# Cross-attention and routed FFN on one core: four PSUM copies of the first two batches moved from ScalarE to VectorE, and one key projection placed behind the transposes

## What is computed

```python
qp = q @ Wq.T                                   # q = layernorm(x)
k, v = jnp.split(latent_kv @ Wkv_expand.T, 2, axis=-1)
scores = jnp.einsum('bhqd,bhkd->bhqk', qh, kh) * inv_sqrt_d
scores = jnp.where(causal, scores, jnp.finfo(scores.dtype).min)
attn = jax.nn.softmax(scores, axis=-1)
out = jnp.einsum('bhqk,bhkd->bhqd', attn, vh)   # heads put together
x = x + out @ Wout.T
x = x + ffn(layernorm(x))                       # top-2 of 8 experts, plus the shared part
```

## Time and profile before

| | us |
|---|---|
| median of 3 runs | 339.84 (339.09 to 340.3) |
| the profiled execution | 340.88 |
| its span, first to last instruction | 339.0 |
| TensorE busy in the span | 323.1 (95%) |
| VectorE busy | 268.6 (79%) |
| ScalarE busy | 232.4 (69%) |
| GpSimd busy | 143.3 (42%) |

### The profile page before, as it was taken

One profiled execution on the slowest core, in us unless ns is written; L12 is line 12 of the kernel. 1 busy time (PEld: TensorE's weight loads), 2 busy tenths in 40 slices (PEclk: granted clock), 3 DMA queues, 4 the chain that ended last, 5 costly groups with the idle time before them and its releaser, 6 DMA issues.

```text
span 339.0 us, 7041 instructions
## 1 busy us (share of the span) xinstructions
PE 323.1 (95%) x2285; PEld 279.3 (82%) x2285; DVE 268.6 (79%) x677; ACT 232.4 (69%) x582; POOL 143.3 (42%) x151
## 2 busy tenths in 40 slices
PE   7999998999999999999999999899999999999990
PEld 7898876777786798889888978789989999999980
DVE  4889779999756176876667998899999999999940
ACT  4666999999844134131225788788899899989830
POOL 3335475888842000352500005557772432432463
PEclk9999999999999999999999999999999999999996
DMA  7999300000005699598699965554455455556243
GB/s 227 380 338 380 139 3 3 3 3 3 0 2 198 248 367 370 237 300 289 224 271 253 251 244 98 102 117 104 90 111 131 90 96 125 114 92 113 50 48 45
DMA packets 32227, 53.03 MB, mean 156 GB/s; under 512 B 7488, under 2 KB 15808, under 8 KB 31168
## 3 DMA queue, kind: packets, MB, share of 16 engines
q1 hardware_dynamic: 24912, 43.31, 39.2%
q0 software_dynamic: 4576, 9.23, 15.9%
q10 hardware_dynamic: 2704, 0.04, 0.5%
HBM read 32.24 MB, written 16.92 MB: 145 GB/s over the span
## 4 chain that ended last, share of the span: by engine, by line
PE 74%; ACT 8%; DVE 5%; DMA 5%; POOL 3%; issue 2%; SPq 1%; POOLq 1%; DVEq 0%; ACTq 0%
PE bank L583 26%; PE bank L913 22%; PE bank L940 5%; ACT prob L1076 4%; PE bank L644 3%; PE bank L944 3%; PE bank L807 2%; PE bank L950 2%; PE bank L954 2%; DMA w_sg<-sguT 2%; DMA act_w<-act_e 2%; DMA w_kv<-wkvT 1%; PE bank L793 1%; PE bank L575 1%; PE bank L655 1%
## 5 line engine op out<-in xcount | busy, mean ns | idle before, releaser
L562 POOL DMA_INDIRECT out<-y_sb,dest x18 | 40.6, 2257 | 91.5 <-ACT y_sb L1256 49.7
L1333 DVE TENSOR_TENSOR gu_parts<-w_gu,gu_parts 128x704 fp32r<-128x704 f32 x84 | 76.0, 939 | 0.4 <-ACT gu_parts L1031 0.2
L1031 ACT ACTIVATE gu_parts<-w_gu 128x704 fp32r x84 | 66.1, 792 | 10.8 <-PE bank L913 9.7
L913 PE MATMUL bank<-gu_parts,xsT_hi 128*128 128x352 f32 x328 | 71.1, 338 | 0.0
L913 PEld LDWEIGHTS bank<-gu_parts,xsT_hi 128*128 128x128 f32 x328 | 54.3, 188 | 5.6 <-issue 4.3
L913 PE MATMUL bank<-gu_parts,xsT_lo 128*128 128x352 f32 x164 | 39.6, 323 | 0.0
L583 PE MATMUL bank<-x2T_hi,w_sg_lo 128*128 128x512 f32 (+1 forms) x88 | 32.6, 371 | 0.1
L583 PE MATMUL bank<-x2T_hi,w_sg_hi 128*128 128x512 f32 (+1 forms) x88 | 31.9, 363 | 0.0
L583 PE MATMUL bank<-x2T_lo,w_sg_hi 128*128 128x512 f32 (+1 forms) x88 | 31.9, 363 | 0.0
L445 POOL TENSOR_TENSOR prob<-prob,rrow 112x448 f32<-112x448 f32 x30 | 27.5, 934 | 9.9 <-DVE rrow L1383 9.8
L523 POOL DMA_INDIRECT xs_dram<-x2n,slot_i x14 | 13.9, 993 | 37.6 <-DVE eid L1631 33.6
(11 more groups left out here) (219 smaller groups left out, 826.3 us busy)
## 6 DMA issues: line engine op xcount, KB each, us to landing
w_gu<-guT SPq DMA_DIRECT2D x8, 1408.0 KB, 9.6
xs_dram<-no_row SPq DMA_DIRECT2D x1, 5460.0 KB, 19.7
xs_in<-xs_dram SPq DMA_DIRECT2D x21, 256.0 KB, 10.1
w_dn<-dnT SPq DMA_DIRECT2D x8, 512.0 KB, 7.9
act_w<-act_e SPq DMA_DIRECT2D x19, 176.0 KB, 2.1
w_sg<-sguT SPq DMA_DIRECT2D x10, 256.0 KB
w_dn<-dnT SPq DMA_DIRECT2D x8, 192.0 KB, 8.5
w_sd<-sdnT SPq DMA_DIRECT2D x5, 256.0 KB, 5.8
```

Source lines behind the costliest of these rows:

```text
L562: pool.indirect_dma_start(out=out[:, :], out_offset=bass.IndirectOffsetOnAxis(ap=dest[:, i, 0:1], axis=0), in_=y_sb[i % 2][:, :], in_offse ...
L913: ins = pe.matmul(dst[:, 0:F], xsT[x_][:, c, :], gu2[w_][:, c, f0:f0 + F], start=c == 0 and n == 0, stop=c == C - 1 and n == 2)
L1031: act.activation(dst, src, ACT.Copy).then_inc(s[sem], 1)
L1333: dve.tensor_tensor(lo_, src, hi_.bitcast(F32), ALU.subtract).then_inc(s[sem], 1)
```

## The change

- wait_probT is written anew: copied_by_vector says which copies VectorE makes, now also (batch 0, row 3), (1, 1) and (1, 3); probT_count works out the count of the copy on its semaphore.
- TensorE: k_proj(1, 2) with its wait for kT(1, 1) goes from ahead of transposed(0, 2) to behind transposed(0, 3).
- ScalarE: loses probT 3 of batch 0, probT 1 and 3 of batch 1, and qT(1, 2).
- VectorE, b = 0: qT(1, 2) ahead of inverse(1, 0); then probT 3 and kT(1, 2), both ahead of masked(1, 3); at the end, between inverse(1, 3) and masked(2, 1), probT 1 of batch 1. b = 1: probT 3 directly behind kT(1, 3).

No instruction is added or left out in sum, and no transfer is touched.

```diff
--- before.py
+++ after.py
@@ -266,6 +266,13 @@
 
         "xin0 xin1 xin2 Tx xs_hi xs_lo gu_hi gu_lo dn_hi dn_lo eg esil eact actw Ta aT_hi aT_lo aT dn_last_hi dn_last edn_split edn ey yst ylo yhi").split()
     s = {n: nc.alloc_semaphore(f"s_{n}") for n in names}
+
+    def copied_by_vector(b, r):
+        return r == 1 if b >= 2 else (b, r) in ((0, 3), (1, 1), (1, 3))
+
+    def probT_count(b, r):
+        by = copied_by_vector(b, r)
+        return sum(copied_by_vector(n // R, n % R) == by for n in range(R * b + r + 1))
 
     token_buffer = lambda i: 2 if i == 2 else 1 if i > 2 and i % 2 == 0 else 0
 
@@ -624,12 +631,7 @@
                 transposes(bank_, x2n[:, n, :]).then_inc(s["T2"], 1)
 
             def wait_probT(b, r):
-                if b < 2:
-                    pe.wait_ge(s["probT"], R * b + r + 1)
-                elif r == 1:
-                    pe.wait_ge(s["probT_v"], b - 1)
-                else:
-                    pe.wait_ge(s["probT"], R * 2 + (R - 1) * (b - 2) + (1 if r == 0 else r))
+                pe.wait_ge(s["probT_v" if copied_by_vector(b, r) else "probT"], probT_count(b, r))
 
             def transposed(b, r):
                 if b == 0 and r < RP:
@@ -753,8 +755,6 @@
                 transposed(b, 1)
                 if b == 0:
                     q_proj(1, 2, D)
-                    pe.wait_ge(s["KT"], C + 2)
-                    k_proj(1, 2, CC)
                 if b == 1:
                     pe.wait_ge(s["QT"], C + 3)
                     q_proj(1, 3, D)
@@ -775,6 +775,9 @@
                 if b >= 3:
                     t2(b - 3, CC)
                 transposed(b, 3)
+                if b == 0:
+                    pe.wait_ge(s["KT"], C + 2)
+                    k_proj(1, 2, CC)
                 if b >= 2:
                     out_proj(b - 2, early, 3 * C)
                 if b + 1 < NB:
@@ -1135,15 +1138,12 @@
                     put_qT(1, 0, D)
             for b in range(NB):
                 put_pT(b, 0)
-                if b < 2:
+                if b == 0:
                     put_pT(b, 1)
                 if b + 1 < NB:
                     exps(b + 1, 0)
-                if b == 0:
-                    put_qT(1, 2, D)
                 if b < 2:
                     put_pT(b, 2)
-                    put_pT(b, 3)
                 if b + 1 < NB:
                     exps(b + 1, 1)
                 if b == NB - 1:
@@ -1478,16 +1478,20 @@
             masked(1, 1)
             masked(1, 2)
             for b in range(NB):
+                if b == 0:
+                    put_qT(2, D)
                 if b == 1:
                     put_kT(3)
+                    put_pT(1, 3)
                 if b + 1 < NB:
                     inverse(b + 1, 0)
+                if b == 0:
+                    put_pT(0, 3)
+                    put_kT(2)
                 if b >= 2:
                     put_pT(b, 1)
                 if b + 1 < NB:
                     masked(b + 1, 3)
-                if b == 0:
-                    put_kT(2)
                 if b == 1:
                     put_qT(3, D)
                 if b + 1 < NB:
@@ -1509,6 +1513,8 @@
                     masked(b + 2, 0)
                 if b + 1 < NB:
                     inverse(b + 1, 3)
+                if b == 0:
+                    put_pT(1, 1)
                 if b + 2 < NB:
                     masked(b + 2, 1)
                     masked(b + 2, 2)
```

## The result

The changed kernel took 337.83 us (median of 4 executions, 337.44 to 338.02) against 339.46 (4 executions): ratio 0.9945, 95% interval 0.9926 to 0.9963. That is 1.63 us less by the medians and 1.9 by the ratio, with 1.3 to 2.5 in the interval. It is faster, and more so than forecast: 338.9 was the forecast, and 337.83 lies 0.07 us under the lower end of the range, 337.9, so the forecast was missed. The profiled execution took 337.44 us, with a span of 335.5.

The account below looks back on a forecast made before the run. ScalarE, full in the first two batches, was taken as the bound through its oT_hi of batch 1. A 1.00 us gain there, cut to 0.90 by waiting for transposes, took 339.84 to 338.9 us; range 337.9 to 340.1.

Parts of the forecast that it names:

- starting value: Median of three runs of the kernel before, 339.84 us, from which the sum subtracted the gain.
- lead: ScalarE's exponentials of batch 2, row 1, start 0.90 us earlier, at 46.24 instead of 47.14; bounds 0.60 to 0.95.
- late part: From the first w_gu load to the end of the span; the 0.90 us shift was to be carried through unchanged.
- Part 1: Batches 0 and 1: the copies taken off ScalarE free about 1.8 us, the upper bound of the gain.
- Part 2: Batch 0: k_proj(1,2) behind the transposes lets them start at 37.36; with the copies moved, ScalarE is 1.00 us ahead.
- Part 3: VectorE's new order ends kT(1,2) at 39.59; batch 0's products start at 39.73, 0.30 us earlier; other delays cost nothing.
- Part 4: Batch 1: ScalarE waits 0.95 us for TensorE's transposes before copying row 2, cutting its 1.00 us to 0.90.
- 0.3 us for runs: Allowance for run-to-run variation, added to the terms' bounds to give 338.6 to 339.5 us.
- (a): GpSimd holds up VectorE's three new probT copies, 0.75 us each: 1.35 us slower, 341.2 us; chance 0.06.
- (b): kT(1,2) comes late, or the gain is lost at the w_sg load near 127.99: 339.3 to 339.8 us; chance 0.20.
- (c): Larger gain: TensorE's 1.5 us act_w wait loosens, 337.4 us, or ScalarE's whole 1.8 us counts, 338.0; chance 0.14.
- (d): Batch 0: ScalarE isn't freed, its copies' time returning as waiting for transposes; no own size, chance counted in (b).

Follow-up runs that it names:

- the repeats: The changed kernel, unchanged, against the kernel before, in three more comparisons of 12 executions each: ratios 0.9970, 0.9964 and 0.9972.

## Why the prediction was right or wrong

The mechanism was right for the first two batches and mis-sized a little; the sum built on it failed, in its starting value, in its lead and in what it allowed for runs. The late part, which it took for unchanged, stays open. Times of after are shifted by 0.27 us, the difference of the first exponentials.

| step | before | forecast | after |
|---|---|---|---|
| products of batch 0 | 40.03 | 39.73 | 39.66 |
| transposes of rows 2, 3, batch 1 | 45.53 | 45.23 | 45.11 |
| copy of row 2, batch 1 | 46.30 | 45.82 | 45.69 |
| exponentials of batch 2, row 1 | 47.14 | 46.24 | 46.13 |
| oT_lo of batch 1 | 50.60 | 49.70 | 49.51 |
| first load of w_gu | 104.67 | 103.77 | 103.62 |

**Part 1, ScalarE: right.** A copy costs 0.43 us of the queue (38.27 to 38.70).

**Part 2, the move: right.** In batch 0 the exponentials after the copy start at 38.43 by before's clock (38.70 - 0.27); 38.42 was forecast. What I didn't say, and the runs showed, is that the move has hardly any value without the copies (0.10 alone, about 0.5 on top).

**Part 3, VectorE: right but for one term.** kT(1,2) ends at 39.60 (39.25 + 0.62 - 0.27; forecast 39.59). The products then start 0.06 us later, not 0.13: that hand-over was taken from a transpose that followed a probT copy and is shorter here. The delays that I costed at nothing cost nothing: batch 1's copy of probT 3 was done before its products, and VectorE gated nothing else.

**Part 4, the wait that takes over: right, 0.15 us too long.** ScalarE waits in batch 1 for the transposes, for 0.80 us (free at 44.83 + 0.33 = 45.16, copy at 45.96), not 0.95, mostly since the transposes are 0.12 earlier. The kernel that moves k_proj(1,3) shows that this was the bound that was left. The step after it, that the shift is carried to the end, held in the timed comparisons within their intervals, and not in the profiled executions, whose late parts differ by 1.5 us in the mean.

**The sum, first term that failed: the lead, 0.90 us, was too small by 0.15 to 0.2.** The stage gave 1.05 in the first pair of traces and 1.1 in the mean of five. 0.12 of the difference is the transposes' earlier start: 0.07 the hand-over, and 0.05 the way from products to transposes, 5.45 instead of 5.50 us (39.93 to 45.38). 0.08 more is a term that the sum put at nothing: ScalarE's oT_hi of batch 1 took 0.55 instead of 0.62 us, and VectorE waits for its end.

**Second and third: the starting value and the 0.3 us for runs.** The sum began at 339.84, a median of three. The same kernel was at 339.46 in the comparison with the result, 0.38 lower, and at 339.3 to 340.0 in the larger ones; the changed one was there at 338.25 to 338.5. So a median of three or four can be off by more than the 0.3 us that the range allowed. The forecast is 0.4 to 0.65 above the larger medians of after, and 1.07 above the first measurement. Of these 1.07, 0.38 is the starting value and 0.2 the lead. The remaining 0.5 is what the first comparison gave beyond the stage (1.63 us, where 36 executions gave 1.05); the repeats point to chance, and a small late gain isn't excluded. The range itself would have held every larger median. The first measurement fell on the faster side, to which I gave 0.36, against 0.58 for no change; an effect of 1.05 us lies just at the 0.3% that I took as the border.

**The rivals.** (a), VectorE's copies held up by GpSimd: no. The copy at 46.43 took 0.61 us beside the w_o passes, and that at 38.66 took 0.60 beside a normalising pass. The Trainium skill's exception (SBUF — State Buffer, Who interferes with whom), a VectorE instruction with at most one input in SBUF and outside the two-port modes, agrees with both rows. (b): no, neither kT(1,2) nor the wait for VectorE's count near 137 cost anything in the profiles of after. (c): in part, in the profiles alone. TensorE's wait for act_w of 1.5 us was absent in the first profile after; by all ten traces it is 0.5 us shorter in the mean, and the times don't show a gain of that kind beyond their intervals. What sets this wait wasn't found. (d): no, but with the copies alone it would have come: there ScalarE waits 0.56 us in batch 0.

## What to carry to other kernels

When work is taken from a full engine, follow the next instruction that waits for another engine: the gain ends there, and if a third engine's queue has independent work ahead of what that instruction waits for, moving the two together gives more than the sum. Here four copies gave 0.6 us, a reordering gave 0.1, and both 1.1. Then look for the same pattern one step on: the twin of the reordering in batch 1 gave another 0.6 us in the traces, for four moved lines and a swap on VectorE. And compare traces stage by stage from a common event: a stage repeated to 0.1 us here, while whole executions of one kernel differ by some 3 us, and a difference of two profiled ones is no measure of a change.

## What the runs showed of the hardware

**In an unbroken queue the tail of ScalarE's instructions grows.** The exponentials that read a bank follow one another every 0.33 us, whatever length the profile gives them, but that length creeps up while ScalarE never waits: in the profile after from 0.39 us at 36.96 to 0.46 at 44.83. Behind the wait that ends at 45.96 it is back at 0.35. The row of oT_hi in batch 1 shows the same. It took 0.53 to 0.55 us in all five traces of after, where ScalarE had waited 0.8 us some three us earlier; 0.62 in all five of before, where the last wait lay over eleven us back; and 0.72 where ScalarE had not waited once since the first exponential (the move alone). Rows of after on both sides of the wait:

```profile
36.96 0.39 ACT L1079 ACTIVATE prob<-bank,negmax 112x112 f32<-112x112 f32 x1
...
44.83 0.46 ACT L1079 ACTIVATE prob<-bank,negmax 112x112 f32<-112x112 f32 x1
...
46.73 0.36 ACT L1079 ACTIVATE prob<-bank,negmax 112x112 f32<-112x112 f32 x1
```

So a short wait on ScalarE cost the instruction that waits for its result up to 0.17 us less than it seems (0.72 against 0.55), and removing one gives that much less. That the growth comes from the missing waits is read off these traces and was not tested by a run of its own.
